# A four-layer graph network on one core: passes over one column half at a time, a GRU inside the passes, norms cut in halves

## What is computed

```python
# layer 0, twice, with relu between: y = adj @ (f[:, None] * (adj @ (y @ W)))
# layer 1
cos = beta * (x @ x.T) / (norm2 @ norm2.T + 1e-07)
P = softmax(cos + (1.0 - adj) * -1e9, axis=1);  return P @ x
# layer 2
msg = relu((adj @ x) @ W_msg.T + b_msg);  return gru_cell(msg, x, W_ih, W_hh, b_ih, b_hh)
# layer 3
deg = clip(sum(adj, axis=1), 1.0);  return x @ W_self + (adj @ x / deg) @ W_neigh
```

## Time and profile before

| | |
|---|---|
| runs | 1759.63, 1757.72, 1752.79 us; median 1757.72 |
| profiled execution | own time 1753.63 us, span in the trace 1751.8 us |
| TensorE matmul (PE) busy | 1656.9 us, 95% of the span |
| TensorE weight load (PEld) | 1389.0 us |
| VectorE (DVE) | 1439.8 us, 82% |
| ScalarE (ACT) | 1242.9 us, 71% |
| GpSimd (POOL) | 397.9 us, 23% |
| loaded and stored | 444.36 MB |
| mean granted clock | 0.976 of full speed |

### The profile page before, as it was taken

One profiled execution on the slowest core, in us unless ns is written; L12 is line 12 of the kernel. 1 busy time (PEld: TensorE's weight loads), 2 busy tenths in 40 slices (PEclk: granted clock), 3 DMA queues, 4 the chain that ended last, 5 costly groups with the idle time before them and its releaser, 6 DMA issues.

```text
span 1751.8 us, 24580 instructions
## 1 busy us (share of the span) xinstructions
PE 1656.9 (95%) x8529; PEld 1389.0 (79%) x8529; DVE 1439.8 (82%) x1537; ACT 1242.9 (71%) x1220; POOL 397.9 (23%) x589
## 2 busy tenths in 40 slices
PE   7999999999998999968999999999879999799995
PEld 6888788888887788847999999999868885388884
DVE  7888888888888888888787778787788886888886
ACT  6777677777777777758778777787567775377766
POOL 1111121111111211123333333333011110022430
PEclk9999999999999999978999999999989999899997
DMA  9999699879986888833333333333468984059993
GB/s 392 388 385 386 239 348 338 337 267 346 337 338 266 322 339 337 317 128 139 145 145 139 134 130 135 138 145 145 193 261 337 340 338 176 1 186 331 334 332 113
DMA packets 60372, 444.36 MB, mean 254 GB/s; under 512 B 6368, under 2 KB 10624, under 8 KB 10752
## 3 DMA queue, kind: packets, MB, share of 16 engines
q1 hardware_dynamic: 60288, 443.36, 67.1%
HBM read 441.23 MB, written 2.11 MB: 253 GB/s over the span
## 4 chain that ended last, share of the span: by engine, by line
PE 84%; DVE 10%; ACT 3%; issue 1%; DMA 1%; POOL 0%; SPq 0%; DVEq 0%; ACTq 0%
PE ps L1014 19%; PE ps L1009 19%; PE ps L1007 19%; PE ps L1083 6%; PE ps L1098 3%; PE ps L1100 3%; PE ps L1069 3%; PE ps L1067 3%; PE ps L1099 3%; PE ps L1068 3%; DVE aL L686 2%; ACT aH L432 2%; DVE xrow L782 1%; DVE ptL L854 1%; DVE yL L690 1%
## 5 line engine op out<-in xcount | busy, mean ns | idle before, releaser
L686 DVE TENSOR_TENSOR aL<-raw,aH 128x2048 fp32r<-128x2048 f32 x336 | 778.2, 2320 | 137.4 <-ACT aH L432 136.7
L432 ACT ACTIVATE aH<-raw 128x2048 fp32r<-128x2048 f32 x336 | 645.7, 1922 | 267.9 <-PE ps L1009 241.5
L1007 PE MATMUL ps<-aH,wH 128*128 128x512 f32 x1536 | 414.7, 392 | 14.5 <-ACT aH L432 10.9
L1014 PE MATMUL ps<-aL,wH 128*128 128x512 f32 x1536 | 413.0, 391 | 3.0 <-DVE aL L686 2.4
L1009 PE MATMUL ps<-aH,wL 128*128 128x512 f32 x1536 | 413.7, 391 | 0.0
L348 POOL CAST wH<-yH 128x128 fp32r (+1 forms) x192 | 146.1, 761 | 993.8 <-PE ps L1014 815.1
L1007 PEld LDWEIGHTS ps<-aH,wH 128*128 128x128 f32 x1536 | 289.2, 189 | 75.8 <-POOL wL L349 10.5
L1014 PEld LDWEIGHTS ps<-aL,wH 128*128 128x128 f32 x1536 | 288.2, 188 | 68.0 <-DVE aL L686 8.5
L1009 PEld LDWEIGHTS ps<-aH,wL 128*128 128x128 f32 x1536 | 290.6, 189 | 60.9
L854 DVE TENSOR_TENSOR ptL<-ps,ptH 128x512 fp32r<-128x512 f32 x256 | 176.5, 689 | 82.4 <-ACT ptH L505 79.7
L376 POOL TENSOR_SCALAR raw<-raw 128x2048 f32<-128x2048 f32 x64 | 122.5, 1914 | 296.8 <-ACT raw L490 296.7
(11 more groups left out here) (122 smaller groups left out, 1521.0 us busy)
## 6 DMA issues: line engine op xcount, KB each, us to landing
raw<-adjT SPq DMA_DIRECT2D x336, 1024.0 KB, 5.2
raw<-adj SPq DMA_DIRECT2D x32, 2048.0 KB, 7.6
kept<-adjT SPq DMA_DIRECT2D x16, 1024.0 KB, 7.9
xrow<-x_rows SPq DMA_DIRECT2D x2, 1024.0 KB, 7.2
xT<-norms SPq DMA_DIRECT2D x1, 2048.0 KB, 7.3
out<-xrow SPq DMA_DIRECT2D x8, 256.0 KB, 3.2
lpar<-late SPq DMA_DIRECT2D x1, 576.0 KB, 11.8
par<-early SPq DMA_DIRECT2D x1, 228.0 KB, 16.9
```

The lines of the kernel that those rows point to most:

```text
L432: nc.scalar.activation(aH[:, h, :], src, ACT.Copy).then_inc(aH_ready, 1)
L686: dve.tensor_tensor(aL[:, h, :], src, aH[:, h, :].bitcast(F32), ALU.subtract).then_inc(aL_ready, 1)
L1007: pe.matmul(b, wH[:, r, :], aH[:, h, c], start=first and r == 0, stop=False)
L1014: ins = pe.matmul(b, wH[:, r, :], aL[:, h, c], start=False, stop=done)
```

## The change

The tiles of a pass go by half first: 32 tiles of columns 0 to 2047, then 32 of the rest. The four banks of the first half are copied, multiplied or turned, filtered and split while the second half multiplies, those of the second half while the first half of the next pass multiplies; each step has a fixed place behind one of the tiles in each engine's program. TensorE reads its weights from `yH` and `yL`, and GpSimd's copies go. Four tiles (`SPLIT_ONCE`) are loaded and split in pass 0 and stay as `onceH` and `onceL` for passes 1 to 3. In passes 4 and 5 four tiles are kept (`KEPT`), loaded once. So 60 of the 64 tiles of passes 1 to 5 go through the ring, or are read again from `kept` in pass 5; pass 0 loads all 64 through it.

Half of norm 1 and of the unit rows is made in the second half of pass 3; in the first super block the masks go in another order (`ORDER0`), and a row's half is loaded by itself. In norm 2 the scales of 24 row blocks come in super block 14; GpSimd normalises six chunks and makes the low part of four; two tiles of pass 4 are split in super block 15; the last two chunks are normalised by ScalarE in pass 4, where all chunks are also turned. The GRU of chunks 0 to 3 lies in the second half of pass 4, of chunks 4 to 7 in the first half of pass 5, each with its norm, its turn and its own share; the mix takes a second sigmoid of the negated argument and three VectorE steps. VectorE adds the own share from PSUM. The first half of the last share, the sums, the scales and the normalisation lie in the second half of pass 5. All loops are written out.

```diff
-    SPAN = NB // 2
-    KEPT_AT = tuple(range(0, 2 * SPAN, 8))
-    NKEPT = 2 * len(KEPT_AT)
+    TILES = 2 * NB
     RING = 4
-    TILES = 2 * NB
+    SPLIT_ONCE = (16, NB + 3, NB + 6, NB + 9)
+    KEPT = tuple(range(0, TILES, 16))
     CH = 1024
     NCH = N // CH
     NSB = NB // 2
     NBATCH = NB // 2
-    FIRST, SECOND = (0, 1), (1, 2)
     LEAD = 4
-    BY_ACT_LAST = (1, 3, 5, 7)
     SCALE_STEPS = 8
-    EARLY_LN = NB - BPB
-    X_NORMALISED_AT = {0: 6, 1: 7}
-    X_SPLIT_AT = {3: 2, 4: 3, 5: 4, 7: 5, 9: 6, 11: 7}
+    EARLY_LN = NB - 2 * BPB
     HIGH_BY_DVE = (1, 7, 11, 15)
+    X_LOADS = ((0, 1), (1, HBK), (HBK, BK))
+    GRU_AT = ((2, 5, 8, 11), (0, 2, 4, 6))
+    NORM_AT = ((11, 17), (8, 12))
+    HIGH_AT = ((15, 16, 21, 22), (12, 13, 16, 17))
+    TURN_AT = (18, 20, 23, 25)
+    SELF_AT = (20, 22, 25, 27)
+    UNIT_AT, X1_AT = (13, 15, 18, 20), (25, 27)
+    X2_LOW_AT = {4: 4, 5: 6, 6: 12, 7: 13}
+    X1_BY_ACT, X2_BY_POOL = 2, 6
+    ORDER0 = tuple((r, 2 * h + i) for h in range(2) for r in range(2) for i in range(2))
...
+    def is_split_once(q, t):
+        return q < 4 and t in SPLIT_ONCE
...
+    ring_tiles = [(q, t) for q, t in split_tiles if not is_kept(q, t)]
+    buf_tiles = [(q, t) for q, t in every_tile if not is_split_once(q, t)]
+    splits_with = {at: n + 1 for n, at in enumerate(split_tiles)}
+    ring_place = {at: n for n, at in enumerate(ring_tiles)}
+    buf_place = {at: n for n, at in enumerate(buf_tiles)}
...
+        def a_tiles(q, t):
+            if is_split_once(q, t):
+                i = SPLIT_ONCE.index(t)
+                return onceH[i][:, :], onceL[i][:, :]
+            slot = buf_place[q, t] % 2
+            return aH[:, slot, :], aL[:, slot, :]
+        def a_before(q, t):
+            if is_split_once(q, t) or buf_place[q, t] < 2:
+                return None
+            return buf_tiles[buf_place[q, t] - 2]
...
+        def masks_of_row(sbi, r):
+            if sbi == 0:
+                return max(n for n, at in enumerate(ORDER0) if at[0] == r) + 1
+            return sbi * 2 * NCH + (r + 1) * NCH
...
+            def load_tile(q, t):
+                s = ring_place[q, t]
+                if s >= RING and (q, t) not in first_after_rows:
+                    sp.wait_ge(aL_ready, splits_with[ring_tiles[s - RING]])
+                sp.dma_start(raw[:, s % RING, :], adjT_tiles[t // NB, t % NB]).then_inc(tile_landed[s % RING], 16)
...
             sp.wait_ge(u_written, 16)
+            sp.wait_ge(proj_done, 4 * BK)
+            sp.wait_ge(unitT_done, BK)
             sp.dma_start(xT[:, 0:N], norms.rearrange("b d -> (b d)").partition_broadcast(D)).then_inc(urow_landed, 16)
             sp.wait_ge(urow_landed, 16)
-            with sp.Fori(1, NSB) as sbi:
...
-                    sp.wait_ge(m_ready, sbi * (2 * NCH) + (r + 1 - 2) * NCH)
+                    sp.wait_ge(m_ready, masks_of_row(sbi - 1, r))
                     sp.dma_start(rowbuf[:, r, :], adj_rows[sbi * 2 + r]).then_inc(row_landed[r], 16)
```

GpSimd, all of it in norm 2 and, ahead of that, in the first super block:

```diff
+            for c in range(X1_BY_ACT, BK):
+                low_of_x(4, c)
+                if c + 2 < BK:
+                    normalise(1, c + 2)
...
+            pool.wait_ge(rstd_ready, 3)
+            for c in range(X2_BY_POOL):
+                normalise(2, c)
+                if c >= 2:
+                    low_of_x(5, c - 2)
```

ScalarE:

```diff
+            def turned_sums(q, b, func=ACT.Copy):
+                wait_bank(act, q, b)
+                if q * BK + b >= HBK:
+                    act.wait_ge(proj_done, q * BK + b - HBK + 1)
+                nc.scalar.activation(turned[b % HBK], ps[:, b, :], func).then_inc(g_ready, 1)
+            def high_of_filtered(q, c):
+                act.wait_ge(z_ready, q * BK + c + 1)
+                act.wait_ge(tile_used, q * TILES + NB + BPB * (c + 1))
+                high(c, filtered[c % HBK])
...
+                for t in range(TILES):
+                    split_high(q, t)
+                    if t < 2 * HBK and t % 2 == 1:
+                        turned_sums(q - 1, HBK + t // 2, ACT.Relu if q - 1 == 1 else ACT.Copy)
+                    if 6 <= t < 6 + 2 * HBK and t % 2 == 0:
+                        high_of_filtered(q - 1, HBK + (t - 6) // 2)
+                    u = t - NB
+                    if 0 <= u and u % 2 == 1 and u < 2 * HBK:
+                        turned_sums(q, u // 2, ACT.Relu if q == 1 else ACT.Copy)
+                    if q < 3 and u >= 6 and (u - 6) % BPB == 0 and (u - 6) // BPB < HBK:
...
+                    c = h * HBK + i
+                    if u == GRU_AT[h][i] + 2:
+                        message(c)
+                    if u == GRU_AT[h][i] + 3:
+                        gates(c)
+                for g in range(2):
+                    if u == NORM_AT[h][g]:
+                        root(4 + 2 * h + g, (h * HBK + 2 * g) * BPB, (h * HBK + 2 * g + 2) * BPB)
+                    if u in (NORM_AT[h][g] + 2, NORM_AT[h][g] + 3):
+                        c = h * HBK + 2 * g + u - NORM_AT[h][g] - 2
+                        act.wait_ge(rstd_ready, 5 + 2 * h + g)
+                        normalise(c, x_by_act)
```

VectorE:

```diff
+            def filtered_rows(q, b):
+                dve.wait_ge(proj_done, q * BK + b + 1)
+                n = q * BK + b
+                if n >= HBK:
+                    dve.wait_ge(yL_ready, BK + n - HBK + 1)
+                if q == 1:
+                    dve.tensor_copy(filtered[b % HBK], ps[:, b, :]).then_inc(z_ready, 1)
+                else:
+                    filt = p("f1" if q == 0 else "f2", b * BPB, (b + 1) * BPB)
+                    dve.tensor_tensor(filtered[b % HBK].rearrange("p (b d) -> p b d", d=D),
+                                      ps[:, b, :].rearrange("p (b d) -> p b d", d=D),
+                                      filt.unsqueeze(2).to_broadcast([D, BPB, D]), ALU.mult).then_inc(z_ready, 1)
...
+                    if q == 0 and t % BPB == 2 and t // BPB + 1 < BK:
+                        low(0, t // BPB + 1, chunk(xrow, t // BPB + 1))
+                    if q == 0 and t == NB:
+                        dve.wait_ge(par_landed, 16)
+                    if q >= 1 and 4 <= t < 4 + 2 * HBK and t % 2 == 0:
+                        filtered_rows(q - 1, HBK + (t - 4) // 2)
+                    if q >= 1 and 7 <= t < 7 + 2 * HBK and t % 2 == 1:
+                        low(q, HBK + (t - 7) // 2, filtered[(t - 7) // 2])
+                    u = t - NB
+                    if q < 3 and 4 <= u < 4 + 2 * HBK and u % 2 == 0:
+                        filtered_rows(q, (u - 4) // 2)
+                    if q < 3 and u >= 7 and (u - 7) % BPB == 0 and (u - 7) // BPB < HBK:
+                        low(q + 1, (u - 7) // BPB, filtered[(u - 7) // BPB])
+                    if q == 3:
+                        if 3 <= u < 3 + 2 * HBK and u % 2 == 1:
+                            c = (u - 3) // 2
+                            turned_rows(c, 3 * BK + c + 1)
...
+            def gru_mix(c):
+                ng, zg = n_s[c % 2], z_s[c % 2]
+                dve.wait_ge(zg_ready, c + 1)
+                dve.scalar_tensor_tensor(out=zg, in0=zg, scalar=1.0, in1=chunk(xT, c), op0=ALU.add,
+                                         op1=ALU.mult).then_inc(carried_ready, 1)
+                dve.wait_ge(rest_ready, c + 1)
                 dve.wait_ge(n_ready, c + 1)
-                dve.tensor_tensor(t, h, ng, ALU.subtract).then_inc(gru_step, 1)
-                dve.wait_ge(gru_step, 3 * c + 1)
-                dve.wait_ge(zg_ready, c + 1)
-                dve.tensor_tensor(t, t, zg, ALU.mult).then_inc(gru_step, 1)
-                dve.wait_ge(gru_step, 3 * c + 2)
-                dve.tensor_tensor(t, t, ng, ALU.add).then_inc(gru_step, 1)
...
+            def gru_steps(h, u):
+                for i in range(HBK):
+                    c = h * HBK + i
+                    if u == GRU_AT[h][i] + 4:
+                        gru_rows(c)
+                    if u == GRU_AT[h][i] + 3:
+                        gru_argument(c)
+                        gru_mix(c)
+                    if u == GRU_AT[h][i] + 5:
+                        bank_stats(c, BK + c + 1)
+                    if u == HIGH_AT[h][i] + 1:
+                        low(6, c, chunk(xrow, c))
+                    if u == SELF_AT[i] + 1:
+                        residual(c)
+                for g in range(2):
+                    lo, hi = (h * HBK + 2 * g) * BPB, (h * HBK + 2 * g + 2) * BPB
+                    value = BK + NB + h * HBK + 2 * g + 2
...
+            def last_rows(c):
+                dve.wait_ge(proj_done, 4 * BK + c + 1)
+                dve.wait_ge(sum_ready, c + 1)
+                for i in range(BPB):
+                    b = c * BPB + i
+                    t = block(xrow, b)
+                    ins = dve.scalar_tensor_tensor(out=t, in0=ps[:, c, i * D:(i + 1) * D], scalar=rdeg[:, b:b + 1], in1=t,
+                                                   op0=ALU.mult, op1=ALU.add)
+                ins.then_inc(t_ready, 1)
```

(95 more changed lines are left out.)

1192 lines of the change are left out of this document (618 added, 574 removed).

## The result

The changed kernel takes 1742.80 us, the median of five runs (1737.76 to 1748.61); the kernel before took 1755.66 in five runs beside it (1752.79 to 1759.63). The ratio is 0.9926, 95% interval 0.9898 to 0.9955: 13 us are gained where 50 were forecast. The profiled execution is the slowest of the five, own time 1748.61 us, span 1746.8, against 1751.8 before: in the two traces the gain is 5.0 us, some 8 less than in the medians.

A forecast was written before the change was run, and what follows sets the result against it. TensorE was taken to bound a pass, so only its waiting could go: gains of 0.9, 7.6, 13.3, 1.5, 7.9, 10.6 and 8.8 sum to 50.6, from 1753.6 to 1703; forecast 1706 us, range 1684 to 1744.

The forecast's parts named there:

- the first block's: First attention block: row 2's late refill and GpSimd's queue cancel norm 1's gain; price 13.3 us, 1719; chance 0.09.
- the ring's: Tile loads: four buffers can't cover landings of 8.0 us, costing 127 us, 1830; decides from 6.6 us on; chance 0.04.
- VectorE rival: Passes 0 to 3 and GRU halves: in-order VectorE holds up splits, 16 to 35 and up to 14 us; chance 0.19.
- Start and joints: Kernel start and joints of passes 0 to 3: gains of 0.9 and 7.6 us, loads costed at nothing.
- Norm 1 and the first block: From pass 3's end to the first attention block's end: 73 us instead of 86.3, gain 13.3.
- Attention: Thirteen middle blocks unchanged at 391 us; last block gains 1.5 us net as GpSimd takes six chunks and two splits come in.
- Pass 4, GRU, tail: Everything behind the attention: gains of 7.9 us into pass 4, 10.6 in the GRU and 8.8 in the tail.
- tables: ScalarE: 14 table loads instead of 6, eight more at 1.28 us, 10.3 us if all show, 1716; chance 0.05.

The follow-up runs named there:

- those two mended: Changed kernel without GpSimd's all-reduce, with norm 1's chunks 4 to 7 normalised on VectorE, ScalarE's order changed, and six buffers in the ring: 1716.39 us, ratio 0.9777.
- The edits on GpSimd and ScalarE: Changed kernel without the all-reduce, chunks 4 to 7 normalised on VectorE, ScalarE reordered: 1721.58 us with four buffers, 1716.39 with six.

## Why the prediction was wrong

- **The mechanism held, two prices failed.** With those two mended the kernel takes 1716.39, still 10 above 1706; that rest is the smaller terms below. The forecast gave each rival a chance alone; the first block's and, in a small size, the ring's came together. The VectorE rival's range, 1716 to 1749, holds the measured time by luck: the profile names 4.9 us of TensorE's waits for VectorE's splits in passes 0 to 3 and 7.1 in passes 4 and 5.
- **Start and joints (8.5 us of gain forecast; 6.6 lost).** The step that failed: "I cost it at nothing; the cover is that 1.4 us." The loads landed in 6.0 to 6.7 us (medians of the traces), not 5.2, when 60 tiles of a pass instead of 56 went through four buffers. The rival had the right place (it "decides from 6.6 us on") and took 8.0 for the landing; its own formula with 6.7 gives (6.7 - 6.6) / 4 x 364 = 9 us. That this comes near is luck: with a median of 6.0 it gives nothing, and such a trace still loses 3.6, as the single late loads count and not the median. The runs give 3.6 to 11.5: 3.6 is the best profiled execution with four buffers against six, 11.5 the changed kernel's; 5.2 is the difference of the medians above. This part is also the one that differs most from run to run. The rest of the miss, 15.1 - 11.5 = 3.6 us, is in the main the difference of two things: the pieces cost TensorE 18.7 us, not 22.1, and the waits behind the start are some 9, not 3. The start held: the sixth tile begins at 26.3 (26.0 forecast), a gain of 0.6 instead of 0.9. Most of the 9 us are at norm 1's pieces: with six buffers pass 3's stretch is still 186 us (551 to 737), where pass 0's fell from 196 to 191.
- **Norm 1 and the first block (13.3 forecast; 6.5 lost).** Two steps failed. "GpSimd's maximum and the flag" stood, with the unit rows, in the 3.3 us between 11 and 14.3: that leaves the instruction little more than its 0.38 us, and nothing for the time around it. In the changed kernel the flag is there 19.1 us behind pass 3, and GpSimd's unit rows 29.7. The trace of before hinted at it: GpSimd's next instruction came 6.9 us behind it, and 3.4 of them lay past the end of the VectorE piece it needed (762.15 to 765.55), though the profile put all to VectorE. Taking it off GpSimd won 12.6 us. And "queued behind GpSimd's low parts and ScalarE's exponents (some 4.5 us)" left out the four normalisations of 3.1 us: row 2's weights were begun at 805.4. The edits on GpSimd and ScalarE bring the block to 72.0 and 73.2, against the forecast's 73; row 2's mask then comes at 39.0 where 41 stood, and 34.3 us follow it where 32 stood, so two misses of some 2 us cancel in the sum. The rival by which this block gains nothing came true in its result and named GpSimd's queue rightly. Its refill was not the cause: it was issued at 789.4 and took some 8 us, and ScalarE's sum at 806.75 waited for no load; in the runs with the short block the refill stands where it stood.
- **Attention (1.5 forecast; 2.2 lost).** Two parts. The block ahead of the last takes 30.4 us instead of 28.8; the scales of 24 row blocks moved into it, and the forecast gave that move no price. The last takes 29.6 instead of 28.5. There the forecast set VectorE's time saved (six chunks) against VectorE's time added (two splits, 4.6 us). VectorE did get less to do, but a split is one piece of 2.3 us, and TensorE waits for what stands behind it: 6.0 us in five waits, where it was 4.8 in ten. The timeline of the last block shows GpSimd normalising a chunk without a split beside it (1273.55) and with one (1277.91), that split, and the matmul that waits behind it:

```profile
1273.55 3.12 POOL L384 TENSOR_SCALAR xrow<-xrow,mean,rstd 128x128 f32<-128x128 f32 x4
...
1277.91 5.15 POOL L384 TENSOR_SCALAR xrow<-xrow,mean,rstd 128x128 f32<-128x128 f32 x4
...
1279.34 2.27 DVE L775 TENSOR_TENSOR aL<-kept,aH 128x2048 fp32r<-128x2048 f32 x1
...
1282.27 0.52 PE L1249 MATMUL ps<-ptH,yH 128*128 128x256 f32 x1 [1.77 <-DVE ptL L953]
```

Behind the split at 1279.34 TensorE waits 1.77 us for VectorE, behind the other 1.53; the longest such wait of the last block before was 1.4. The forecast added 1.07 us to a split beside GpSimd; these took 2.27 and 2.44, and GpSimd lost the time. This is read from the trace alone; no run moved the splits or the scales.
- **Pass 4, GRU, tail (27.3 forecast; 20.3 won).** Pass 4 starts as the attention ends (1292.8), the tail is 18.3 us, the GRU's chunks cost TensorE their 6.5 us. Of 87.5 us that passes 4 and 5 (217.5 and 218.2, about 209 each forecast) are longer than 128 tiles, the forecast's own terms for what TensorE works on there are 66.0 for the GRU and 3.8 for norm 2's turns: 18 us of stalls, where 2 and 8 were taken. By the starts of the tiles, some 14 of them lie between 1452 and 1502 and between 1564 and 1628, where norm 3's scales, turns and own shares stand; at the GRU's own pieces there are next to none. The profile names only the 7.1 us of waits for VectorE's splits, in 17 of 128 tiles, and 1.1 for ScalarE's copies. The longest of them shows VectorE's order in the timeline, as the VectorE rival had it (up to 14 us):

```profile
1459.12 0.17 DVE L829 TENSOR_TENSOR s<-s 128x8 f32<-128x8 f32 x1
...
1459.20 2.29 DVE L775 TENSOR_TENSOR aL<-raw,aH 128x2048 fp32r<-128x2048 f32 x1
...
1459.32 0.21 ACT L505 ACTIVATE s<-s 128x8 f32<-128x8 f32 x1 [1.58 <-DVE s L829]
...
1461.55 1.20 PE L1155 MATMUL ps<-aL,yH 128*128 128x512 f32 x4 [1.49 <-DVE aL L775]
```

VectorE's scale steps (to 1459.2) stand ahead of the tile's split, which ends at 1461.5; ScalarE waits 1.58 us for the same steps, TensorE 1.49 for the split. It isn't tables. No run took these steps out, so how much of the 18 us they are is open.
- **A sum.** The VectorE rival's 1716 to 1749 are counted from 1700; 16 to 35 and up to 14 us on the forecast of 1706 are 1722 to 1755.
- **Right:** 2.72 us a tile with weights straight from `yH` and `yL`, as two neighbours in pass 3 show; no subtract of 3.36 us in a pass (360 take 2.29 in the mean); the joints are gone; 391 us for the blocks in the middle; the tail.

```profile
744.49 1.07 PE L1150 MATMUL ps<-aH,yL 128*128 128x512 f32 x4
...
747.21 1.07 PE L1150 MATMUL ps<-aH,yL 128*128 128x512 f32 x4
```

## What to carry to other kernels

A ring is sized by what the load takes when the ring alone feeds the engine, not by what it took beside buffers of its own: here medians of 6.0 to 6.7 us against a slack of 6.6 cost 3.6 to 11.5 us, and two more buffers in place of one split tile were worth 5.2. So when the measured landing time comes near the slack, count the slack as used up, and look for more buffers before memory goes to keeping one more tile split. Work that is moved to an idle engine is priced with that engine's own durations and in its own order: look for whoever stands behind it in the queue. And an instruction whose bar stands between two unexplained gaps, as the all-reduce's does, is priced by the time from the end of the one before to the start of the one behind, less what it would have waited anyhow (13.6 us by the trace; taking it out won 12.6).

## What the runs showed of the hardware

Around the all-reduce GpSimd stands still for 5.8 us ahead and 7.7 us behind, with no instruction shown; five other traces that keep it have 5.6 to 5.9 ahead and 7.0 to 7.5 behind. Before, 8.1 us of idle time lay ahead of it in any case. The Trainium skill (GPSIMD Engine Reference, section "2.1 Instruction dispatch") says that the first call of a freshly loaded routine pays for loading its code, about 6 us, with no visible instruction. The first gap agrees in size, though no run shows that it is such a load; of the second it says nothing.

Beside a VectorE split that reads two SBUF tiles GpSimd's four normalisations of a chunk took 5.15 us (1277.91), without it 3.12 (1273.55): GpSimd lost 2.0 of the split's 2.27 us and VectorE nothing; beside the other split it lost 1.7, VectorE 0.15. In the kernel before it was VectorE that lost 1.07. The Trainium skill (SBUF — State Buffer, section "Who interferes with whom") has the two exclude each other, which both agree with; which of them waits differed.

One core took 393 GB/s over the 191 us of pass 0 with six buffers, and 369 over 196 with four.
